# Quantised inner rows of a feed-forward block: transposed by DMA, not by TensorE

## The reference

```python
x = x + tanh(g_xattn[0]) * L0_xattn(layernorm(x), ctx)
x = x + tanh(g_ffn[0])   * L0_ffn(layernorm(x))      # this one
x = x + tanh(g_xattn[1]) * L1_xattn(layernorm(x), ctx)
x = x + tanh(g_ffn[1])   * L1_ffn(layernorm(x))
# L0_ffn: D = 512, F = 1376
xq   = fake_quant_act(x)           # per row: scale = amax/127, whole numbers -127..127
h    = silu(xq @ Wg.T) * (xq @ Wu.T)
out  = fake_quant_act(h) @ fake_quant_weight(Wd).T
```

## Time and profile before

| what | value |
|---|---|
| time, median of three | 774.05 us |
| profiled execution, its own time | 774.1 us |
| its span (first to last instruction) | 772.3 us |
| TensorE busy | 747.4 us, 97% of the span |
| VectorE, ScalarE, GpSimd busy | 77%, 63%, 65% |

### The profile page before, as it was taken

The page is one execution under the profiler, slowest core; times in us unless marked ns, Lnnn a source line. Parts: engine busy times, 40 slices in busy tenths (PEclk is TensorE's granted clock), DMA queues, the critical chain, the costliest instruction groups (busy, mean ns, idle before and its releaser), DMA issues.

```text
span 772.3 us, 13671 instructions
## 1 busy us (share of the span) xinstructions
PE 747.4 (97%) x4829; PEld 593.8 (77%) x4829; DVE 592.6 (77%) x1138; ACT 489.7 (63%) x1082; POOL 498.3 (65%) x431
## 2 busy tenths in 40 slices
PE   8989899999999999999999999998899999999997
PEld 7867688888788888888878888775666777787776
DVE  5877878867788776678776666776999997898873
ACT  5754756666666545565555655344689898888772
POOL 2685777556766875556884557734477877787762
PEclk9998999999999999999999999999999999999999
DMA  9310454433454122351214201363263333122101
GB/s 338 116 68 28 105 108 110 137 83 82 111 131 116 51 97 62 88 141 56 69 48 101 82 1 33 60 261 137 62 158 97 96 88 92 35 64 62 48 17 41
DMA packets 74640, 71.03 MB, mean 92 GB/s; under 512 B 48412, under 2 KB 49660, under 8 KB 74188
## 3 DMA queue, kind: packets, MB, share of 16 engines
q1 hardware_dynamic: 74284, 69.82, 32.4%
q10 hardware_dynamic: 288, 0.33, 0.1%
HBM read 49.04 MB, written 6.34 MB: 72 GB/s over the span
## 4 chain that ended last, share of the span: by engine, by line
PE 85%; DVE 7%; POOL 3%; ACT 3%; issue 1%; DMA 1%; DVEq 0%
PE bank L81 12%; PE bank L83 11%; PE bank L82 11%; PE bank L588 6%; PE bank L593 6%; PE bank L589 6%; PE bank L672 4%; PE bank L570 4%; PE bank L1731 4%; PE bank L1717 3%; PE bank L1683 2%; PE bank L1654 2%; PE bank L1662 2%; PE bank L1707 2%; PE bank L1708 2%; POOL rope_swap L1295 1%
## 5 line engine op out<-in xcount | busy, mean ns | idle before, releaser
L1295 POOL TENSOR_TENSOR rope_swap<-rope_swap,trig 128x512 f32<-128x512 f32 x80 | 104.8, 1310 | 145.1 <-ACT rope_swap L758 145.1
L1031 DVE SCALAR_TENSOR_TENSOR x_res<-bank,gate,x_res 128x512 f32<-128x512 f32 x128 | 95.2, 745 | 55.2 <-PE bank L593 54.7
L885 ACT CAST oT_hi<-bank 128x512 fp32r<-128x512 f32 x64 | 34.4, 590 | 131.5 <-PE bank L672 131.5
L588 PE MATMUL bank<-wo_hi,oT_hi 128*128 128x512 f32 x256 | 101.9, 398 | 5.4 <-DVE x_res L1031 4.9
L81 PE MATMUL bank<-xnT_hi,wq_hi 128*128 128x512 f32 x252 | 101.5, 403 | 0.0
L589 PE MATMUL bank<-wo_lo,oT_hi 128*128 128x512 f32 x256 | 100.6, 393 | 0.0
L83 PE MATMUL bank<-xnT_hi,wq_lo 128*128 128x512 f32 x252 | 100.0, 397 | 0.0
L82 PE MATMUL bank<-xnT_lo,wq_hi 128*128 128x512 f32 x252 | 99.5, 395 | 0.0
L1301 POOL TENSOR_TENSOR q_rope<-rope_cos,rope_swap 128x512 f32<-128x512 f32 x64 | 82.9, 1295 | 5.0
L593 PE MATMUL bank<-wo_hi,oT_lo 128*128 128x512 f32 x256 | 80.0, 394 | 4.1 <-DVE oT_lo L1185 4.1
L3075 POOL TENSOR_TENSOR b_e<-b_e,b_inv 128x512 f32<-128x512 f32 x64 | 68.3, 1081 | 18.9 <-DVE b_inv L2268 18.4
(11 more groups left out here) (277 smaller groups left out, 1957.3 us busy)
## 6 DMA issues: line engine op xcount, KB each, us to landing
wq_raw<-in_wq_tiles SPq DMA_DIRECT2D x16, 512.0 KB, 3.7
wo_raw<-in_L_xattn_wo SPq DMA_DIRECT2D x16, 512.0 KB, 4.1
xn<-in_L_ffn_Wd SPq DMA_DIRECT2D x16, 256.0 KB, 2.8
b_ctx<-in_ctx SPq DMA_DIRECT2D x32, 128.0 KB, 2.6
b_k_twice<-b_qk_hi SPq DMA_DIRECT2D x32, 128.0 KB, 2.4
w_T_dram<-w_out SPq DMA_DIRECT2D x28, 128.0 KB, 3.1
w_T<-w_T_dram SPq DMA_DIRECT2D x2, 1376.0 KB, 9.8
xn<-in_L_ffn_Wg SPq DMA_DIRECT2D x10, 256.0 KB, 4.0
```

The source lines that it names most:

```text
L588: pe.matmul(out, oT_hi[:, tl, h], wo_hi[jp][:, h, :], start=(h == 0), stop=False)
L1031: dve.scalar_tensor_tensor(out=K.x[:, t, :], in0=wo_ps[t % 2][:, :], scalar=K.gate[:, 0:1], in1=K.x[:, t, :], op0=ALU.mult, op1=ALU.add).t ...
L1295: pool.tensor_tensor(out=sw, in0=sw, in1=sin_b, op=ALU.mult).then_inc(s_rope, 1)
```

## The change

For tiles 1 to 7 ScalarE's `h_shifted` adds another constant, and three new ScalarE instructions `h_int(t, n)` behind it subtract it again and write bf16 whole numbers to `M.hq`. SyncE issues three DMA transposes, one for each column group, from `M.hq` into `hqT`. TensorE's transposes of these tiles and ScalarE's copies out of PSUM are gone. Tile 0 is done as before. `down(t)` waits for the three transfers; the steps of TensorE that waited for the copies out of PSUM (since they write the same banks) wait for the readers of the banks before them.

```diff
             def down(t):
-                pe.wait_ge(s_hTa_sb, t + 1)
-                pe.wait_ge(s_hTb_sb, t + 1)
+                if t == 0:
+                    pe.wait_ge(s_hT_sb, 2)
+                else:
+                    pe.wait_ge(s_hT, 16 * NFG * t)
...
             attend_pair(0, 0)
-            pe.wait_ge(s_gate, 8)
-            h_transpose_a(1)
             logits(1, 6)
-            pe.wait_ge(s_up, 8)
-            h_transpose_b(1)
             weights_T(1, 1)
...
             def h_shifted(t):
                 act.wait_ge(s_hs, 4 * t + 3)
+                magic = MAGIC_HALF if t == 0 else MAGIC
+                act.activation(h[t % 2][:, :], h[t % 2][:, :], ACT.Copy, bias=magic, scale=h_inv[t % 2][:, :]).then_inc(s_hq, 1)
+
+            def h_int(t, n):
+                lo, w = FGROUPS[n]
+                act.wait_ge(s_hq, t + 1)
+                if t > 1:
+                    act.wait_ge(s_hT, 16 * NFG * (t - 1))
+                if t == 1 and w % P:
+                    act.copy(M.hq[n][:, w:], h[t % 2][:, 0:P - FL])
+                act.activation(M.hq[n][:, 0:w], h[t % 2][:, lo:lo + w], ACT.Copy, bias=-MAGIC).then_inc(s_h_int, 1)
...
             h_shifted(1)
+            h_int(1, 0)
+            h_int(1, 1)
+            h_int(1, 2)
             exps(1, 4)
             copy_T(1, 0)
-            hT_copy_a(1)
             split_hi(4, 0)
             copy_T(1, 1)
             exps(1, 5)
-            hT_copy_b(1)
...
+            def turn_h(t):
+                sp.wait_ge(s_down, t)
+                for n, (lo, w) in enumerate(FGROUPS):
+                    c, k = lo // P, -(-w // P)
+                    sp.wait_ge(s_h_int, NFG * (t - 1) + n + 1)
+                    sp.dma_start_transpose(hqT[:, c:c + k, :], M.hq[n][:, 0:k * P]).then_inc(s_hT, 16)
...
             load_ctx(4, 0)
+            turn_h(1)
             load_ctx(5, 1)
...
             load_ctx(7, 1)
+            turn_h(5)
             duplicate(6, 1)
```

More of the change, by code:

```diff
@@ L1517, in late_buffers @@
     M.low_w = take("l1_low", [P, DC, P + E_ACT])
+    hq_wide = take("f_hq_wide", [P, FGROUPS[2][0]], BF16)
+    late.used = at["q_rope0"] + 4 * (D + DC * P // 2 + 2 * D)
+    hq_rest = take("f_hq_rest", [P, (FT - 2 * DC) * P], BF16)
+    assert late.used <= at["q_rope1"]
+    M.hq = [hq_wide[:, 0:D], hq_wide[:, D:2 * D], hq_rest]
     M.bT = M.e[0]
@@ L1663, in up_mm, with h_transpose_a, h_transpose_b @@
                 mm.then_inc(s_up_ps, 1)
-            def h_transpose_a(t):
-                pe.wait_ge(s_hq, t + 1)
+            def h_transpose_a():
+                pe.wait_ge(s_hq, 1)
                 for c in range(8):
[L1668 to L1672, removed]
+                    mm = pe.transpose(hT_a[:, c, :], low_half(h[0])[:, c * P:(c + 1) * P], K.ident_b[:, :])
+                mm.then_inc(s_hT_ps, 1)
+            def h_transpose_b():
+                pe.wait_ge(s_hq, 1)
                 for c in range(8, FT):
                     w = P if c < FT - 1 else FL
-                    mm = pe.transpose(hT_b[0:w, c - 8, :], low_half(h[t % 2])[:, c * P:c * P + w], K.ident_b[:, :])
-                mm.then_inc(s_hTb, 1)
+                    mm = pe.transpose(hT_b[0:w, c - 8, :], low_half(h[0])[:, c * P:c * P + w], K.ident_b[:, :])
+                mm.then_inc(s_hT_ps, 1)
             def down(t):
-                pe.wait_ge(s_hTa_sb, t + 1)
-                pe.wait_ge(s_hTb_sb, t + 1)
+                if t == 0:
+                    pe.wait_ge(s_hT_sb, 2)
+                else:
+                    pe.wait_ge(s_hT, 16 * NFG * t)
                 for c in range(FT):
@@ L1742, in x3_T @@
                 if t == NT - 1:
-                    pe.wait_ge(s_hTb_sb, NT)
+                    pe.wait_ge(s_up, NFG * NT)
                 else:
@@ L1841, in tensor @@
             pe.wait_ge(s_up, 5)
-            h_transpose_b(0)
+            h_transpose_b()
             pe.wait_ge(s_gate, 6)
-            h_transpose_a(0)
+            h_transpose_a()
             pe.wait_ge(s_qk_lo[1], 3)
             qk(2, 0)
-            pe.wait_ge(s_hTb_sb, 1)
+            pe.wait_ge(s_hT_sb, 1)
             up_mm(1, 2)
             weights_T(0, 5)
-            pe.wait_ge(s_hTa_sb, 1)
+            pe.wait_ge(s_hT_sb, 2)
             down(0)
@@ L1883, in tensor @@
             weights_T(1, 2)
-            pe.wait_ge(s_hTa_sb, 2)
+            pe.wait_ge(s_gate, 8)
             gate_mm(2, 2)
             logits(1, 7)
-            pe.wait_ge(s_hTb_sb, 2)
+            pe.wait_ge(s_up, 8)
             up_mm(2, 2)
@@ L1964, in tensor @@
             logits(3, 4)
-            pe.wait_ge(s_hTa_sb, 4)
+            pe.wait_ge(s_gate, 12)
             gate_mm(4, 0)
@@ L1973, in tensor @@
             weights_T(3, 2)
-            pe.wait_ge(s_hTb_sb, 4)
+            pe.wait_ge(s_up, 12)
             up_mm(4, 0)
@@ L2075, in tensor @@
             logits(5, 7)
-            pe.wait_ge(s_hTa_sb, 6)
+            pe.wait_ge(s_gate, 20)
             down(5)
@@ L2120, in tensor @@
             x3_T(4)
-            pe.wait_ge(s_hTa_sb, 7)
+            pe.wait_ge(s_gate, 23)
             gate_mm(7, 2)
             logits(6, 7)
-            pe.wait_ge(s_hTb_sb, 7)
+            pe.wait_ge(s_up, 23)
             up_mm(7, 2)
@@ L2157, in tensor @@
             logits(7, 6)
-            pe.wait_ge(s_hTa_sb, 8)
+            pe.wait_ge(s_out, 7)
             down(7)
@@ L2212, in make_h @@
                 m, (lo, w) = NFG * t + n, FGROUPS[n]
-                if n == 0:
-                    after(dve, s_hTa, t - 1)
-                    after(dve, s_hTb, t - 1)
+                if n == 0 and t == 2:
+                    dve.wait_ge(s_hT_ps, 2)
+                if n == 0 and t > 2:
+                    dve.wait_ge(s_h_int, NFG * (t - 2))
                 dve.wait_ge(s_tanh, m + 1)
@@ L2682, in h_shifted, with hT_copy_a, hT_copy_b @@
                 act.wait_ge(s_hs, 4 * t + 3)
[L2683 to L2692, removed]
+                magic = MAGIC_HALF if t == 0 else MAGIC
[8 more added lines that the diff above has]
+                act.activation(M.hq[n][:, 0:w], h[t % 2][:, lo:lo + w], ACT.Copy, bias=-MAGIC).then_inc(s_h_int, 1)
+            def hT_copy_a():
+                act.wait_ge(s_hT_ps, 2)
+                act.activation(hqT[:, 0:8, :], hT_a.bitcast(FP16), ACT.Copy, bias=-HALF_ZERO).then_inc(s_hT_sb, 1)
+            def hT_copy_b():
+                act.wait_ge(s_hT_ps, 1)
                 act.activation(hqT[:, 8:FT - 1, :], hT_b[:, 0:FT - 9, :].bitcast(FP16), ACT.Copy, bias=-HALF_ZERO)
-                act.activation(hqT[0:FL, FT - 1, :], hT_b[0:FL, FT - 9, :].bitcast(FP16), ACT.Copy, bias=-HALF_ZERO).then_inc(s_hTb_sb, 1)
+                act.activation(hqT[0:FL, FT - 1, :], hT_b[0:FL, FT - 9, :].bitcast(FP16), ACT.Copy, bias=-HALF_ZERO).then_inc(s_hT_sb, 1)
             def hi_qk(t, par):
@@ L2804, in scalar @@
             copy_T(0, 4)
-            hT_copy_b(0)
-            hT_copy_a(0)
+            hT_copy_b()
+            hT_copy_a()
             hi_qk(2, 0)
@@ L2857, in scalar @@
             h_shifted(2)
+            h_int(2, 0)
+            h_int(2, 1)
+            h_int(2, 2)
             exps(2, 3)
-            hT_copy_b(2)
             split_hi(5, 0)
             copy_T(2, 0)
-            hT_copy_a(2)
             hi_qk(4, 0)
@@ L2888, in scalar @@
             h_shifted(3)
+            h_int(3, 0)
+            h_int(3, 1)
+            h_int(3, 2)
             x3_copy(1)
             exps(3, 2)
-            hT_copy_a(3)
             xT_copy(4)
@@ L2927, in scalar @@
             h_shifted(4)
+            h_int(4, 0)
+            h_int(4, 1)
+            h_int(4, 2)
             copy_T(4, 0)
@@ L2964, in scalar @@
             h_shifted(5)
+            h_int(5, 0)
+            h_int(5, 1)
+            h_int(5, 2)
             copy_T(5, 1)
             exps(5, 5)
-            hT_copy_b(5)
             tanh_half(6, 0)
@@ L2998, in scalar @@
             h_shifted(6)
+            h_int(6, 0)
+            h_int(6, 1)
+            h_int(6, 2)
             exps(6, 4)
@@ L3025, in scalar @@
             h_shifted(7)
+            h_int(7, 0)
+            h_int(7, 1)
+            h_int(7, 2)
             route_exp(5)
@@ L3307, in sync @@
             duplicate(3, 0)
+            turn_h(2)
             duplicate(4, 0)
@@ L3312, in sync @@
             load_ctx(6, 1)
+            turn_h(3)
             duplicate(5, 0)
@@ L3315, in sync @@
             store(1)
+            turn_h(4)
             load_ctx(7, 0)
@@ L3321, in sync @@
             duplicate(7, 0)
+            turn_h(6)
             store(3)
@@ L3324, in sync @@
             store(4)
+            turn_h(7)
             store(5)
```

46 lines of the change are left out of this document (7 added, 39 removed).

## The result

The changed kernel takes 775.73 us (median of 20 runs, 774.03 to 777.99), the kernel before in the same runs 774.05 us (772.94 to 775.6). The ratio is 1.0025, 95% interval 1.0017 to 1.0032: about 0.25% slower, a small loss whose interval is clear of 1. A later pair of the two gave 1.0018 (1.0008 to 1.0028). The forecast was 774.9 us within 771.6 to 779.4.

What follows compares the result with a forecast made beforehand. TensorE was taken to bound the kernel, busy 192.82 of 195 us. 774.1 - 4.3 (transposes) + 1.55 (tile 1) + 1.6 (tile 2) + 1.3 (tile 4) + 0.7 (tile 7) = 774.95, given as 774.9 us, range 771.6 to 779.4.

Steps and rivals of the forecast that it cites:

- Transposes, -4.3 us: TensorE, tiles 1 to 7: taking out seven times 8 + 3 transposes saves 0.61 us a tile, 4.3 us.
- the smoother joints: TensorE's steps on either side of the removed transposes might run together better: 0 to 0.8 us, taken as 0.
- ScalarE's block, 1.56 us behind h_shifted: ScalarE: the three new h_int make everything behind h_shifted come 1.56 us later.
- Tile 1, 1.55 us: TensorE before logits(1, 6): exps(1, 4) on ScalarE comes late, a stall of 1.55 us.
- Tile 2, 1.6 us: TensorE before down(2): 5.42 us of room for the transposed rows, so a stall of 1.6 us.
- Tile 3, none: TensorE before down(3): 7.2 us of room, so no stall, or 0.4 us with the slower landing.
- Tile 7, 0.7 us: TensorE before down(7): 6.3 us of room for the transposed rows, so a stall of 0.7 us.
- The bounds of 3 to 7: Test of the whole prediction: wrong if TensorE's brackets from 567 to 762 us sum below 3 or above 7 us.
- hqT is whole at s + 7.0: All transposed rows have landed and TensorE is awake 7.0 us (or 7.6) after h_shifted starts.
- ScalarE's waits are hidden: Rival: ScalarE makes up its lag before TensorE asks, only tiles 2 and 7 pay: 772.1 us, faster; chance 0.25.
- the three transposes get in each other's way: Rival: slower issues and landing, rows whole about 8.4 us after h_shifted starts: 779.4 us, slower; chance 0.17.
- the block is paid in every tile: Rival: each of the seven tiles costs ScalarE's 1.56 us: 780.7 us; chance 0.06.

Runs made afterwards that it cites:

- e1: The changed kernel without the h_int steps and DMA transposes, down(t) of tiles 1 to 7 multiplying tile 0's rows: 769.72 us, kernel before 773.92.
- e2: The changed kernel with every h_int but no DMA transposes, down(t) multiplying tile 0's rows: 773.06 us, kernel before 773.92.
- e10: The changed kernel with only tile 1's h_int moved behind exps(1, 4) and copy_T(1, 0): 774.73 us, kernel before 774.17.
- e5: The changed kernel with all transfers, but down(t) of tiles 1 to 7 doesn't wait and reads a slice of the weights: 773.15 us, kernel before 773.92.
- e4: The changed kernel with two DMA transposes a tile (1024 and 384 columns) in place of three: 773.71 us, kernel before 773.48.
- e8: The changed kernel with the two context loads ahead of tile 3's transposes put behind them: one run of 777.83 us.

## Why the prediction was right, step by step

- *Transposes, -4.3 us.* e1: 4.2 us between the medians, and 2.95 in TensorE's list plus 1.0 of new waits for ScalarE. Right as a price; the smoother joints, taken as 0, are not seen.
- *ScalarE's block, 1.56 us behind h_shifted.* copy_T(4, 0) starts 2.92 us after its h_shifted (forecast 2.91), exps(1, 4) 3.04 (3.06). Right.
- *Tile 1, 1.55 us.* 1.60 (0.99 + 0.61), bracket 1.50. e2 has it without transfers and e10 loses it by order alone: right, and its cause shown.
- *Tile 2, 1.6 us.* 1.87. e5 shows that without the wait the tile stands at -0.36, so 1.62 of it is the wait for the transfer.
- *Tile 3, none.* 0.64. **Wrong.**
- *Tile 4, 1.3 us.* 1.25, in brackets of 0.54 and 0.46, also in e2.
- *Tiles 5 and 6, none.* -0.06 and 0.07.
- *Tile 7, 0.7 us.* 1.11, of which brackets of 0.18 and 0.19 are for copy_T and 0.37 for the transfer.
- *duplicate(6, 1) hidden with 0.4 us of room.* Hidden, with 0.1.

The stalls sum to 6.5 us where the forecast had 5.15. The bounds of 3 to 7 were set for TensorE's brackets in the stretch; these sum to 6.9, close under the upper one, and 2.1 of that stood in the kernel before, whose rows the prediction took to be without brackets. That held around the tiles that it read.

All the excess of 1.3 is one mis-sized term: that hqT is whole at s + 7.0. The forecast had the third issue start at s + 4.65 and 2.35 us for its landing and TensorE's wake. It started at s + 4.72 in tile 2, 5.34 in tile 3 and 4.91 in tile 7, and down started 2.52 to 2.54 us behind it: 2.39 for the landing where the forecast had 2.3, and 0.14 for the wake where it had 0.05, a number with no row behind it. That makes s + 7.25, 7.88 and 7.43, and stalls of 1.83, 0.7 and 1.1 us. (The table agrees with these to 0.04 us, which proves little, since both count the distance from h_shifted to down.) The greater part of the excess is the long issues, 1.82 us in tile 3 and 1.44 in tile 7. An issue of 2.05 us stood in the earlier trace rows, and I had given it to a rival alone, as if either all issues were long or none.

Of the rivals, that ScalarE's waits are hidden is refuted by e2. That the three transposes get in each other's way is refuted as a rule (four of seven tiles issue at 1.25 and land at 2.4 to 2.5) and true in part: its sign, a wait of down(3), is there. That the block is paid in every tile is refuted by tiles 5 and 6. The forecast lies 0.8 us under the median, and that is in part luck. TensorE's list came out 1.3 us longer than forecast (2.19 against a net of 0.85), which on 774.1 would be 776.3; the median lies 0.6 under that, within the gap told above whose cause is open.

## What to carry to other kernels

Work that is taken from the busiest engine and given to one with 17% idle time can still cost more than it saves, because what counts is the few tenths of a microsecond between the other engine's next result and its reader: place the new block behind the results that are awaited, and check each tile's distance from producer to consumer against the whole latency of the new path. Here that latency was 7.25 us at best (write, three issues, landing), and up to 7.9 with a long issue, so tiles with less room should keep the old way; a mixed kernel was faster than either pure one. And time won is worth something only if the next wait doesn't swallow it, as tile 2 swallowed tile 1's. Where a transfer is issued in pieces to start it early, compare the piece's issue time with what the early start gains: two issues beat three.

## What the runs showed of the hardware

- The issue of a DMA transpose from SBUF to SBUF holds SyncE about 1.25 us at each of the sizes used: 1.23 to 1.36 for 128x1024 and 1.25 to 1.27 for 128x384 in e4, 1.19 to 1.28 for 128x512 where it isn't a long one. The plain copies of the same 128 KB as a 128x512 transpose are issued in 0.5 to 0.6 us.
- Landing of 128x512, from the start of the issue, is 2.4 us at best and 2.5 in the median, against 2.4 for the plain copies; 128x1024 lands after 3.2 to 3.3 us in e4. The Trainium skill says in "Advanced Engine Details and Errata", X-Bar Transpose (TRN2), that transposing DMAs are as fast as regular ones. By landing the trace agrees for 128 KB; by the time of the issuing queue, which decided here, it doesn't.
- Some issues take 1.4 to 2.4 us. In every profile with three transposes a tile they fell in tiles 1, 3 and 7 only and never in 2, 4, 5 and 6 (2.50 to 2.54 for two issues, always); not all of the three are long in each profile. With two transposes a tile the wide one takes 1.28 to 1.55 there. e8 rules out the two loads before tile 3. All 19 issues of the transposes of h above 1.4 us overlap a 16 KB packet of the profile's instruction queue; that this packet is the cause is likely and not shown.
- TensorE transposes of 128x128 bf16 that follow one another cost 52 ns each (e1), though one lasts 219 ns.
